# Attention and sixteen experts: the experts' two parts cut at five and three batches in place of four and four

## What is computed

```python
q, k = elu(x @ Wq + bq) + 1, elu(x @ Wk + bk) + 1          # 16 heads of 16
attn = q @ (k^T v)                                          # linear attention, per batch and head
x = layernorm(x + (sigmoid(x @ Wg + bg) * attn) @ Wo + bo)
scores = softmax(x @ gate_w.T)                              # 16 experts in 4 groups
# the 2 best groups, in them the 4 best experts of each token, c = their scores
y = sum over the 4 experts e: c[e] * ((silu(x @ w1[e]) * (x @ w3[e])) @ w2[e])
z = (silu(x @ ws1) * (x @ ws3)) @ ws2                       # the shared expert, 256 wide
out = layernorm(x + y + z)
```

## Time and profile before

| | |
|---|---|
| three timed runs | 701.73, 698.48, 703.09 us; median 701.73 |
| profiled execution | 698.33 us, of it the span 696.5 us |
| TensorE matmuls | 517.0 us busy (74%) |
| VectorE | 427.1 us (61%) |
| ScalarE | 300.6 us (43%) |
| GpSimd | 290.6 us (42%) |
| transfers | 118.63 MB, mean 170 GB/s |
| TensorE's clock, mean | 0.925 of 2.4 GHz |

### The profile page before, as it was taken

One profiled execution on the slowest core, in us unless ns is written; L12 is line 12 of the kernel. 1 busy time (PEld: TensorE's weight loads), 2 busy tenths in 40 slices (PEclk: granted clock), 3 DMA queues, 4 the chain that ended last, 5 costly groups with the idle time before them and its releaser, 6 DMA issues.

```text
span 696.5 us, 13485 instructions
## 1 busy us (share of the span) xinstructions
PE 517.0 (74%) x3554; PEld 355.2 (51%) x3555; DVE 427.1 (61%) x1200; ACT 300.6 (43%) x659; POOL 290.6 (42%) x334
## 2 busy tenths in 40 slices
PE   1899886789897787888886787888887779782300
PEld 1355543455454356676674566676765666441100
DVE  2447783777755877557654344366757657585384
ACT  2536644446334252555554555355645446121000
POOL 1000126365455421545644200634435450787664
PEclk9999999799999989999999999899999999997555
DMA  7022338285561302677767776677777763334232
GB/s 193 25 76 77 124 118 288 75 274 192 202 225 54 113 31 69 220 231 241 252 243 247 252 226 210 189 232 226 222 246 230 240 198 137 99 120 123 83 113 98
DMA packets 64091, 118.63 MB, mean 170 GB/s; under 512 B 9760, under 2 KB 23088, under 8 KB 64048
## 3 DMA queue, kind: packets, MB, share of 16 engines
q1 hardware_dynamic: 51216, 84.55, 37.2%
q0 software_dynamic: 12288, 33.57, 15.4%
q10 hardware_dynamic: 544, 0.00, 0.0%
HBM read 55.17 MB, written 62.91 MB: 170 GB/s over the span
## 4 chain that ended last, share of the span: by engine, by line
PE 35%; issue 17%; DVE 17%; SPq 8%; POOL 7%; ACT 5%; DMA 5%; another core or an unknown queue 5%; DVEq 0%; ACTq 0%; POOLq 0%
PE t L1340 4%; PE h_even L1149 3%; PE h_even L1151 3%; PE h_even L1150 3%; PE h_odd L1149 3%; PE h_odd L1151 3%; PE h_odd L1150 3%; DMA kv<-expert_in 2%; PE y L1186 2%; SPq L327 2%; POOL q_fm L452 2%; SPq L330 2%; POOL wa_stage L452 2%; POOL gate L452 2%
## 5 line engine op out<-in xcount | busy, mean ns | idle before, releaser
L440 POOL DMA_INDIRECT expert_in<-x_all,slots x128 | 132.9, 1038 | 111.7 <-PE h_odd L1151 45.1
L1340 PE MATMUL t<-ident,kv 128*128 128x128 f32 x384 | 61.7, 283 | 23.8 <-DMA kv<-expert_in 16.6
L452 POOL DMA_INDIRECT wa_stage<-expert_out,result_of x64 | 62.9, 982 | 28.2 <-issue 17.5
L452 POOL DMA_INDIRECT q_fm<-expert_out,result_of x32 | 32.1, 1003 | 89.8 <-DMA expert_out<-q_exp 64.1
L1044 DVE TENSOR_TENSOR wa_lo<-bias_heads,wa_hi 128x256 bf16<-128x256 f32 x96 | 40.5, 422 | 46.6 <-ACT wa_hi L642 37.2
L426 POOL TENSOR_SCALAR neg_mean<-mv 128x4 f32<-128x4 f32 x16 | 4.6, 290 | 148.7 <-DVE mv L699 148.5
L1340 PEld LDWEIGHTS t<-ident,kv 128*128 128x128 f32 x384 | 44.9, 145 | 33.8 <-issue 17.6
L1025 DVE TENSOR_TENSOR xsT_lo<-t,xsT_hi 128x512 bf16<-128x512 f32 x72 | 49.4, 688 | 13.2 <-ACT xsT_hi L617 6.6
L1150 PE MATMUL h_even<-xsT_lo,we_hi 128*128 128x256 bf16 x192 | 53.6, 279 | 2.2 <-issue 2.2
L1149 PE MATMUL h_even<-xsT_hi,we_hi 128*128 128x256 f16 x192 | 53.5, 279 | 1.8 <-DVE bias_heads L1036 1.3
L1151 PE MATMUL h_even<-xsT_hi,we_lo 128*128 128x256 f16 x192 | 53.6, 279 | 1.2 <-issue 1.1
(11 more groups left out here) (222 smaller groups left out, 1522.0 us busy)
## 6 DMA issues: line engine op xcount, KB each, us to landing
kv<-expert_in SPq DMA_DIRECT2D x96, 256.0 KB
expert_out<-k_exp SPq DMA_DIRECT2D x48, 256.0 KB
expert_out<-q_exp SPq DMA_DIRECT2D x48, 256.0 KB
expert_in<-wa_stage SPq DMA_DIRECT2D x16, 512.0 KB
expert_in<-wa_stage SPq DMA_DIRECT2D x32, 256.0 KB
stage<-in_L_ffn_w SPq DMA_DIRECT2D x48, 128.0 KB
x_in<-in_L_attn_x SPq DMA_DIRECT2D x8, 512.0 KB
out<-gated SPq DMA_DIRECT2D x8, 512.0 KB
```

The costliest lines, as they stand in the source:

```text
L440: pool.indirect_dma_start(xs_dram[b // WB], bass.IndirectOffsetOnAxis(ap=slots[:, b, t, j:j + 1], axis=0), x_all[:, b, t, :], None).then_i ...
L452: pool.indirect_dma_start(y_got[i][:, j, :], None, ys_dram[w], bass.IndirectOffsetOnAxis(ap=result_of[:, b, t, j:j + 1], axis=0)).then_inc ...
L1340: last = pe.transpose(t_bank[r % 2][:, c * 2 * P + i * P:c * 2 * P + (i + 1) * P], xs[r][:, i, c * P:(c + 1) * P], ident[:, :])
```

## The change

The parts are five and three batches: 56 and 40 pairs, still 96. The attention stage scatters four rows of `dispatch` at a time (20 tiles, 80 scatters, all of part 0), and VectorE writes part 0's region ends a batch later. In part 0, 48 scatters follow, four after each four pairs, and SP's clearing keeps groups 7 to 10, now of 14. Part 0 has 20 tiles to gather behind it. VectorE adds 18 of them, 72 sums, at an even pace over pairs 6 to 39 of part 1, with the three written batches at pairs 16, 23 and 31. In the tail 14 tiles are left to add and 12 to gather. There GpSimd has the normalizations of batches 3 and 4 in a row behind batch 5's gathers. The loops of VectorE over the second part's pairs are written out.

```diff
-    WB = NB // WAVES
-    WT = WB * TT
-    NPAIR = WT * TOP_K // 2 + E
+    BATCHES = (5, 3)
+    START = (0, BATCHES[0], NB)
+    TILES = [TT * n for n in BATCHES]
+    NPAIR = [n * TOP_K // 2 + E for n in TILES]
+    FIRST = (0, NPAIR[0])
-    EARLY = WB - 1
+    EARLY = 3
+    SUM_PAIRS = (6, 40)
+    SUMMED = 18
+    NORM_PAIR = (16, 23, 31)
...
-SPREAD = 3
+SPREAD = 4
@@ SP
-            with sp.Fori(3, (last - 1) // 2) as q2:
+            with sp.Fori(3, 5) as q2:
                 group(0, 2 * q2 + 1, fill=E + 2 * RING * (q2 - 3))
                 group(0, 2 * q2 + 2, fill=E + 2 * RING * (q2 - 3) + RING)
+            for q in range(11, last):
+                group(0, q)
@@ GpSimd
-                if 0 < k < WT:
-                    pool.wait_ge(h_ready, NPAIR + (3 * k if k < WT - TT else 3 * WT - 13 + 2 * (k - WT + TT)))
+                if w == 0 and k > 0:
+                    pool.wait_ge(h_ready, FIRST[1] + 17 * k // 9)
...
-            for i in range(WT):
+            for i in range(TILES[1]):
                 if i > 0:
-                    pool.wait_ge(h_ready, 5 * i // 2)
+                    pool.wait_ge(h_ready, 4 * i)
...
-                        if b > 0 and t == (1 if w == 0 else TT - 1):
+                        if w == 0 and t == TT - 2 and 0 < b <= EARLY:
                             rstd_of(NB + b - 1)
+                    if w == 1:
+                        for ln in range(EARLY if b == START[1] else b - 1, b):
+                            rstd_of(NB + ln)
@@ VectorE
-            batch(5, True, True, True, early=PAIRS - 1, plan=True)
-            batch(6, True, True, True)
+            batch(5, True, True, True, early=PAIRS - 1)
+            batch(6, True, True, True, plan=True)
...
-            group(q1)
-            for i in range(3):
-                group(q1 + 1 + i, 0, thirds[i])
-            with dve.Fori(1, EARLY) as b:
-                group(q1 + 1 + 3 * b, b, thirds[0])
-                group(q1 + 2 + 3 * b, b, thirds[1], norm=b - 1)
-                group(q1 + 3 + 3 * b, b, thirds[2])
-            group(q1 + 1 + 3 * EARLY, EARLY, halves[0], whole=False)
-            group(q1 + 2 + 3 * EARLY, EARLY, halves[1], norm=EARLY - 1, whole=False, last=True)
+            sums = [[] for p in range(NPAIR[1])]
+            for i in range(SUMMED * TOP_K):
+                at = SUM_PAIRS[0] + i * (SUM_PAIRS[1] - SUM_PAIRS[0]) // (SUMMED * TOP_K)
+                sums[at].append((i // (TT * TOP_K), i // TOP_K % TT, i % TOP_K))
+            norms = {NORM_PAIR[b] + t: (b, t) for b in range(EARLY) for t in range(TT)}
+            for p in range(NPAIR[1]):
+                pair(FIRST[1] + p, p % RING, p < NPAIR[1] - 2, sums[p], norms.get(p))
-            tiles = [(b, t) for b in range(WB, NB) for t in range(TT)]
+            tiles = [(0 if k < TILES[0] else 1, k // TT, k % TT) for k in range(SUMMED, NB * TT)]
...
-            for par in range(SHARED):
-                shared_hidden(SHARED * EARLY + par)
-            for n in range(WB, NB):
-                at = 2 * (n - WB)
+            for n in range(EARLY, NB):
+                at = SHARED * (n - EARLY)
                 shared_hidden(SHARED * n, tiles[at])
                 shared_hidden(SHARED * n + 1, tiles[at + 1])
-                add_shared(n - 1, WT + at + 2)
-                dve.wait_ge(shared_added, n)
-                if n in (WB + 1, WB + 2):
-                    whole_norm(n - 2)
-                if n < WB + 2:
+                if n > EARLY:
+                    add_shared(n - 1, SUMMED + at + 2)
+                    dve.wait_ge(shared_added, n)
+                    if n > EARLY + 1:
+                        whole_norm(n - 2)
                     whole_stats(n - 1)
-            whole_stats(WB + 1)
-            add_shared(NB - 1, WT + 2 * WB)
+            add_shared(NB - 1, SUMMED + SHARED * (NB - EARLY))
```

More of the change, by code:

```diff
@@ L353, in _ @@
             sp.wait_ge(rows_ready, 1)
-            for b in range(WB):
+            for b in range(BATCHES[0]):
                 sp.wait_ge(dispatched[b], 16 * TT * TOP_K)
@@ L383, in _ @@
                 group(1, 2 * q2)
-            group(1, 5)
             store_out(0)
-            for q in range(6, 9):
+            for q in range(5, 7):
                 group(1, q)
             store_out(1)
-            for q in range(9, last):
+            for q in range(7, last1):
                 group(1, q)
             for r in range(-3, RING):
-                store_ys(1, RING * last + r, r % RING)
-            with sp.Fori(WB - 2, NB) as b:
+                store_ys(1, RING * last1 + r, r % RING)
+            with sp.Fori(EARLY - 1, NB) as b:
                 store_out(b)
@@ L939, in batch @@
                 if plan:
-                    count_region(0, WB - 1)
+                    count_region(0, BATCHES[0] - 1)
             xt_lo(0)
@@ L987, in shared_hidden @@
                 if add:
-                    combine(1, *add, 0, whole=False)
+                    combine(*add, 0)
                 dve.wait_ge(a_hi_ready, g + 1)
@@ L992, in shared_hidden @@
                     for j in range(1, TOP_K):
-                        combine(1, *add, j, whole=False)
+                        combine(*add, j)
             def add_shared(n, tiles_seen=0):
@@ L1026, in xst_lo, with pair @@
                                   xsT_hi[r][:, :, :], ALU.subtract).then_inc(xst_lo_ready, 1)
-            def pair(g, r, ahead=True, add=None, norm=None, whole=True, part=None):
+            def pair(g, r, ahead=True, add=(), norm=None, part=None):
                 if ahead:
@@ L1037, in pair @@
                 if add:
-                    combine(0, *add[0], whole)
+                    combine(0, *add[0])
                 if norm is not None:
-                    final_norm(norm, r)
+                    final_norm(*norm)
                 if part:
@@ L1044, in pair, with combine @@
                 dve.tensor_tensor(aT_lo[r % 2][:, :], a_pair, aT_hi[r % 2][:, :], ALU.subtract).then_inc(at_lo_ready, 1)
-                if add and len(add) > 1:
-                    combine(0, *add[1], whole)
-            def combine(w, b, t, j, whole=True):
+                for some in add[1:]:
+                    combine(0, *some)
+            def combine(w, b, t, j):
                 if j == 0:
                     dve.wait_ge(y_gathered[t], 16 * TOP_K * (b + 1))
-                if late(b, 1) or t > 0 or j > 0:
+                if b > 0 or t > 0 or j > 0:
                     dve.wait_ge(combined, TOP_K * (TT * b + t) + j)
@@ L1073, in final_norm, with group @@
                     last.then_inc(out_ready, 1)
-            def group(q, b=None, tiles=(), norm=None, whole=True, parts=(), last=False):
+            def group(q, parts=()):
                 for r in range(RING):
-                    add = [(b, i // TOP_K, i % TOP_K) for i in tiles[r]] if tiles else None
-                    pair(RING * q + r, r, not (last and r >= 2), add, norm, whole,
-                         parts[r] if r < len(parts) else None)
-            q1 = GROUPS_OF_PAIRS
+                    pair(RING * q + r, r, part=parts[r] if r < len(parts) else None)
+            q1 = PAIR_GROUPS[0]
             xst_lo(0, 0)
```

103 lines of the change are left out of this document (53 added, 50 removed).

## The result

The changed kernel takes 734.12 us in the median of four executions (732.76, 733.82 and 734.43, and one of 1288.92 that the ratio leaves out and that nothing here explains) against 702.08: **4.6% longer**, ratio 1.046 with a 95% interval of 1.041 to 1.051. The profiled execution has a span of 731.0 us against 696.5, 34.5 more.

A forecast was written before the change was run, and what follows sets the result against it. It saw attention bound by waits across engines, pairs not by VectorE, the tail mostly by GpSimd's gathers. Attention +1.0, pairs -2.3, tail -14.0 sum to -15.3: 683.0 us, scaled to 686.4; range 677 to 699.

The forecast's parts named there:

- 0.23 us a scatter: Part one, pairs beside region ends: the added cost of a scatter in each pair, giving 3.52 us a pair.
- Scatters in fours, +1.0 us: Attention stage: four more scatters a batch fit GpSimd's idle time; larger table and transfers add +1.0 us, bounds 0 and +3.0.
- Part one, 172.7 us: First 56 pairs: 28 with thinner scatters 80.4 us, 16 with region ends 56.3, 12 with neither 36.0.
- Part two, 134.5 us: Last 40 pairs: first four 18.8 us, 36 at 3.12 us each, plus 3.4 us for denser VectorE sums.
- exposed share: Part two: VectorE's added sums mostly hide behind TensorE, costing 0.1 us a pair, 3.4 us in 34; bounds 0 and 10.5.
- the 3.5: Part two: a pace past 3.5 us a pair would show the prediction wrong.
- The tail, -14.0 us: After the last pair: 12 tiles to gather instead of 16; -14 us, taken between -17 and -9.
- the walk without the hole: Tail: the new order walked with old durations, ending at 680 against 696.5, so -17 us.
- the hole: Tail: add_shared's idle 7.88 us without a releaser; if it comes again in full, -9 us, 691.4 us in all, chance 0.18.
- The slower one: Rival, part two: VectorE bounds 34 pairs at 3.76 us each, +21.8 us instead of +3.4; 709.8 us, chance 0.08.
- The rival on slower launches: Tail: GpSimd's gathers slow to 1.37 us beside denser sums, adding 20.6 us; 707.1 us, chance 0.02.

The follow-up runs named there:

- 643 level: Not a run: the faster of two session levels, where the kernel before takes 643 to 644 us; numbers are compared within a level only.
- edited forms: The changed kernel with half the gathers, half-column gathers, one-column sums or scatters in threes; at the 643 level part two took 107 to 111 us.
- 700 level: Not a run: the slower of two session levels, where the kernel before takes 698 to 711 us in the median.
- half of the gathers: The changed kernel without every second gather of part 0's first 18 tiles; part two took 120 us at the 700 level, 106.7 (repeated: 107.4) at the 643 level.
- short sums: The changed kernel with the 72 sums among the pairs cut to one column; part two took 164 us at the 700 level, 110.0 at the 643 level.
- the one with threes: The changed kernel with the attention stage's scatters in threes instead of fours; 645.26 us, ratio 1.005 to the kernel before, at the 643 level.

## Why the prediction was wrong

The failed step is in two terms, and it is one step: GpSimd's launches in the attention stage and in part two were costed by GpSimd's own time, and not by what a run of them takes from TensorE. Only part one had a price for them, 0.23 us a scatter, from the rows.

- **Scatters in fours, +1.0 us.** The argument was that GpSimd idled 7.07 us and gets 5.1 more. That was right for GpSimd: it still idles ahead of its normalizations (2.5 to 6.0 us in batches 3 to 6). But the stage grew by 22.3, because during the longer runs TensorE's results reach the others late; 11 to 14 of it come with fours alone, by the kernel before with this one edit.
- **Part one, 172.7 us.** Measured 173.0, in part by luck: the first 28 pairs took 84.1 us for 80.4, the 16 beside region ends 55.9 for 56.3, the last 12 33.0 for 36.0. Scatters in four pairs instead of two and a half brought no relief (3.00 us a pair as before), and the 12 pairs without them ran faster than taken, 2.40 to 2.96 us as means of four.
- **Part two, 134.5 us.** Measured 166.5, and this is the whole miss of the pairs (-2.3 forecast, +30.6 measured). VectorE's busy time was right: 82.6 us from 502.7 to 635.7, the 34 pairs with sums, so 2.43 a pair where 2.44 was forecast. Its exposed share, taken as 3.4 us, is not measured by itself; half of the sums' time gone brought 3.6 us, within the spread of the traces. Missing was the term for the launches, put at nothing: GpSimd puts 80 of them into this stretch, in runs mostly of 8 and one of 16, where it put 64, mostly in runs of 4 and two of 8. 36 launches fewer bring 43 us back. The range of this term went from VectorE hidden to VectorE in full, and no bound was on GpSimd. The pace of 4.2 us a pair is past the 3.5 that the prediction named as a sign of being wrong.
- **The tail, -14.0 us.** -18.5 from the last silu, and 17.1 us less behind the first gather (88.4 for 105.5), as the walk without the hole gave, though most of the hole is there again (5.36 of 7.88 us). Long runs of launches cost little here: at the 643 level the tail of the changed kernel's edited forms with all gathers takes 96.0 to 97.4 us, against 95.2 to 98.4 for the changed kernel at the 700 level.
- **Rivals.** The slower one, VectorE as the bound at 3.76 us a pair, named a time of 709.8 and the wrong engine: the 39 steps from silu to silu take 4.29 us each with the full sums and 4.20 with the short ones (167.4 and 163.8 us). The rival on slower launches also falls: the gathers of tiles 2 and 3 average 973 ns (982 in the earlier trace rows), so the slowing that the Trainium skill describes (SBUF — State Buffer, section "SBUF: two separate sides": a DMA issued from GpSimd that takes far longer beside certain VectorE copies) is not what happened; here the launches keep their length and the others wait.

What a launch costs at the 700 level, an estimate from the traces of both levels: of stretches with the same code, the difference of their times over the launches in them at the 700 level. TensorE's lower clock is in it.

| stretch | 700 | 643 | launches | us each |
|---|---|---|---|---|
| fours in the kernel before, pairs of part one | 155.6 | 137.6 | 60 | 0.30 |
| the same, part two | 156.0 | 129.8 | 64 | 0.41 |
| half of the gathers, part two | 120.0 | 107.0 | 44 | 0.30 |
| short sums, part two | 163.8 | 108.7 | 80 | 0.69 |
| changed kernel and edited forms, attention stage | 298.2 | 269.0 | 84 | 0.35 |
| the same, part one | 173.7 | 157.0 | 44 | 0.38 |

The cost is 0.3 to 0.4 us in five of the stretches and 0.69 in the changed kernel's part two. The length of the runs alone doesn't explain this, since the attention stage has runs of 12 and 16 and costs 0.35. The pace may, or how much else can go on while TensorE waits; no run separates them, since the launches of part two were never spaced out at an unchanged count. Nor is it known what in the chip holds TensorE, why a machine is at one level or the other (chip 13 by the record was at both), and what the changed kernel takes at the 643 level. Every execution of the experiments comes with a clock read from its trace, so it is open, too, whether the recording has a part in the waits.

## What to carry to other kernels

Launches of indirect DMAs are not free because GpSimd is idle: count them per stretch, and look at what TensorE's consumers wait for while a run of them goes on. A wait in the trace of before that has no releaser ("remote", "issue") is a term of the sum that wants a cause before work of its kind is made denser; here two such waits stood in the rows, the pairs at 4.70 us and the 7.88 us ahead of `add_shared`. And where the baseline itself takes one time today and another tomorrow, compare only within a session: at the 643 level this change may well be a gain, by the estimate above.

## What the runs showed of the hardware

- The kernel before on one chip (13) took 644 us in one session and 710 in the next. The launches are as long at both levels (means of 0.99 to 1.02 us over a kernel), and the packets of the larger queue take about as long (261 us in the changed kernel at the 700 level, 255 us in the one with threes at the 643 level). The waits that set the levels apart begin 2 to 11 us into a run of indirect-DMA launches in the changed kernel's trace, and end inside it or some 3 us behind it at the latest. Until the first launch, at 102 us, the levels agree.
- In such a run TensorE's matmuls of 256 columns started 2.10 us apart (493.17 to 499.47) in place of 0.11 to 0.21, and VectorE's wait for a group of matmuls that is recorded as done ended 13.5 us late (112.4 to 125.92).
- Halving the bytes of 72 gathers at an unchanged number of launches changed the time of part two by nothing that can be told (168.2 against 163.4 to 169.0 us); leaving 36 launches out took 43 us off it (163.4 to 120.0).
